# Row gathers that drop padding places by a bounds check, in a two-layer graph network on one core

## What is computed

```
h = relu(layernorm(x))                            # layer 0: attention, 2 heads of 64
feat = (h @ W).reshape(N, 2, 64)
e = leaky_relu(el[src] + er[dst]); alpha = softmax of e over the edges of one dst
x = x + layernorm(segment_sum(feat[src] * alpha, dst) + bias)
h = relu(layernorm(x))                            # layer 1: three hops
agg = h
for _ in range(3):
    att = sum((agg[head] @ q_w) * tanh(rel * agg[tail] @ k_w))     # head = src, tail = dst
    agg = normalized segment_sum(softmax(att) * rel * agg[tail], head)
    out = out + agg + h
x = x + out
```

## Time and profile before

| | |
|---|---|
| median of 3 runs | 9552.52 us (9550.24 to 9559.58) |
| the profiled execution: its own time, its span | 9554.53 us, 9552.7 us |
| busy share of the span, PE / DVE / ACT / POOL | 84% / 81% / 78% / 71% |
| row gathers on POOL | 6832 indirect DMAs |
| DMA engines, mean busy share in the hops | 0.54 |

### The profile page before, as it was taken

How to read it: one execution, slowest core, us unless ns; L and a number is a source line. 1 busy time by engine, 2 the same in 40 slices (tenths; PEclk the granted TensorE clock), 3 DMA queues, 4 the chain that set the end, 5 groups by cost and what they waited for, 6 DMA issues and landing times.

```text
span 9552.7 us, 271679 instructions
## 1 busy us (share of the span) xinstructions
PE 7999.1 (84%) x62097; PEld 6935.3 (73%) x62097; DVE 7758.0 (81%) x33664; ACT 7498.1 (78%) x24462; POOL 6812.7 (71%) x7069
## 2 busy tenths in 40 slices
PE   8977777777776888888887888888887888888887
PEld 7866666666665777777776777777776777777776
DVE  8989999999997777777777777777777777777776
ACT  6739999999986777777777777777777777777776
POOL 2347777777775777777776777777776777777776
PEclk9989999999998999999998999999998999999999
DMA  2014444444444555555555555555555555555555
GB/s 55 5 35 108 108 108 110 108 108 108 108 113 132 157 161 156 159 157 158 161 155 167 157 158 159 157 161 156 159 159 163 161 156 159 158 158 161 156 160 147
DMA packets 1127114, 1309.11 MB, mean 137 GB/s; under 512 B 446660, under 2 KB 840730, under 8 KB 1126716
## 3 DMA queue, kind: packets, MB, share of 16 engines
q1 hardware_dynamic: 896038, 843.26, 28.7%
q0 software_dynamic: 229264, 460.98, 19.0%
q10 hardware_dynamic: 1670, 3.16, 0.1%
HBM read 1041.61 MB, written 261.38 MB: 136 GB/s over the span
## 4 chain that ended last, share of the span: by engine, by line
PE 35%; DMA 21%; issue 15%; DVE 12%; POOL 10%; ACT 4%; SPq 1%; DVEq 1%; POOLq 0%; ACTq 0%
PE bank L782 27%; DMA agg<-agg_d,arena 18%; POOL agg L744 10%; PE bank L959 3%; PE bank L944 3%; PE bank L912 2%; DVE agg L1689 2%; DVE agg L1679 2%; DVE arena L1788 2%; ACT arena L1100 2%; DMA agg<-feat_d,arena 1%; ACT arena L1180 1%; DVE arena L1765 1%; DVE arena L1669 1%; DVE arena L1647 1%
## 5 line engine op out<-in xcount | busy, mean ns | idle before, releaser
L744 POOL DMA_INDIRECT agg<-agg_d,arena x5124 | 4871.6, 951 | 1687.1 <-issue 1380.6
L1788 DVE TENSOR_TENSOR arena<-agg,bank 128x256 f32<-128x256 f32 x2562 | 1079.8, 421 | 1404.7 <-DMA agg<-agg_d,arena 1184.5
L782 PE MATMUL bank<-arena 128*128 128x129 f32 x10248 | 1763.1, 295 | 305.1 <-ACT arena L1180 297.8
L744 POOL DMA_INDIRECT agg<-feat_d,arena x1708 | 1619.5, 948 | 532.1 <-issue 418.5
L782 PEld LDWEIGHTS bank<-arena 128*128 128x128 f32 x10248 | 1378.9, 195 | 434.5 <-issue 409.4
L1176 ACT ACTIVATE arena<-arena 128x1 f32<-128x1 f32 x2562 | 755.4, 295 | 1158.1 <-DVE arena L1653 1121.8
L782 PE MATMUL bank<-tmp,wide 128*128 128x256 f32 x5124 | 1577.9, 391 | 6.4 <-DMA wide<-left_d 6.4
L782 PE MATMUL bank<-tmp,kw_s 128*128 128x256 f32 x5124 | 1567.3, 388 | 0.1
L959 PE MATMUL bank<-ident,arena 128*128 128x128 f32 x5124 | 1027.3, 283 | 509.6 <-DVE arena L1788 506.6
L959 PEld LDWEIGHTS bank<-ident,arena 128*128 128x128 f32 x5124 | 695.4, 144 | 932.4 <-DVE arena L1788 709.3
L1171 ACT ACTIVATE arena<-agg,arena 128x256 f32<-128x256 f32 x2562 | 1342.4, 524 | 17.6 <-DVE arena L1781 12.1
(11 more groups left out here) (251 smaller groups left out, 16728.2 us busy)
## 6 DMA issues: line engine op xcount, KB each, us to landing
state_d<-arena SPq DMA_DIRECT2D x488, 455.0 KB
arena<-key_d SPq DMA_DIRECT2D x489, 448.0 KB
arena<-type_d SPq DMA_DIRECT2D x367, 448.0 KB
wide<-left_d SPq DMA_DIRECT2D x2562, 64.0 KB
agg<-agg_d,arena POOLq DMA_INDIRECT x5124
agg<-feat_d,arena POOLq DMA_INDIRECT x1708
arena<-er_d SPq DMA_DIRECT2D x854, 1.0 KB
arena<-peers SPq DMA_DIRECT2D x489, 7.0 KB
```

The lines of the kernel that those rows point to most:

```text
L744: nc.gpsimd.indirect_dma_start(out=rows_r[:, k % R, c, 0:width], out_offset=None, in_=table, in_offset=bass.IndirectOffsetOnAxis(ap=peer_r ...
L782: return nc.tensor.matmul(out, lhsT, rhs, start=start, stop=stop)
L1788: V.tensor_tensor(val_r[:, j % R, :, 0:F], rows_r[:, j % R, :, 0:F], bank[0][:, 0:G].rearrange("p (c f) -> p c f", c=2), ALU.mult).then_in ...
```

## The change

Padding places that are put behind the edges keep a real peer in one place of eight (KEPT = 8). In the other seven the peer field is filled with ones, which gives peer 8191, beyond the last node 6249. The row gathers get a bounds check at N - 1 that drops such rows instead of reporting an error. `decode` no longer clamps the peer number to 6249. The 86 padding places of layer 0 hold peer 7168 and are dropped too. A dropped row leaves in `rows_r` what stood there; a memset of the whole ring, once, makes that finite.

```
+KEPT = 8
+        filler_made = sem("filler_made")
+        filler_spread = sem("filler_spread")
...
-            sp.wait_ge(rowid_made, 1)
+            sp.wait_ge(filler_spread, 2)
             sp.dma_start(sorted_edges[0][WINDOWS * G:].rearrange("(l w) o -> l (w o)", l=1), sentinel[:, 0:G]).then_inc(prefilled, 16)
             sp.dma_start(sorted_edges[1][NB * REGION:NB * REGION + G].rearrange("(l w) o -> l (w o)", l=1), filler[0:1, :]).then_inc(prefilled, 16)
...
+            sp.wait_ge(rowid_made, 1)
             for at in range(0, U * SW, NG):
...
                         nc.gpsimd.indirect_dma_start(
                             out=rows_r[:, k % R, c, 0:width], out_offset=None, in_=table,
                             in_offset=bass.IndirectOffsetOnAxis(ap=peer_r[:, k, c:c + 1], axis=0),
+                            bounds_check=N - 1, oob_is_err=False,
                         ).then_inc(q["gathered"][k % R], 16)
...
             V.tensor_copy(iota16[:], colid[:, 0:CAP])
+            dve.wait_ge(filler_made, 2)
+            for i in range(1, KEPT):
+                last = V.tensor_scalar(filler[:, i:G:KEPT], filler[:, i:G:KEPT], MASK, None, ALU.bitwise_or)
+            last.then_inc(filler_spread, 1)
+            for i in range(1, KEPT):
+                last = V.tensor_scalar(sentinel[:, i:G:KEPT], sentinel[:, i:G:KEPT], MASK, None, ALU.bitwise_or)
+            last.then_inc(filler_spread, 1)
...
-                    do(V.tensor_scalar(s_peer, s_field, float(N - 1), None, ALU.min))
+                    do(V.tensor_copy(s_peer, s_field))
...
-                    do(V.tensor_scalar(s_peer, s_other, float(N - 1), None, ALU.min))
+                    do(V.tensor_copy(s_peer, s_other))
...
                 if s == 0:
+                    do(V.memset(rows_r, 0.0))
                     do(V.memset(acc_r[:, U - 1:U, :], 0.0))
```

More of the change, by code:

```diff
@@ L589, in _ @@
             nc.gpsimd.iota(giota[:], [[1, NG]], base=0, channel_multiplier=0, allow_small_or_imprecise_dtypes=True)
-            nc.gpsimd.iota(filler[:], [[1, G]], base=0, channel_multiplier=STRIDE)
-            nc.gpsimd.iota(sentinel, [[1, G]], base=PADKEY << SHIFT, channel_multiplier=0)
+            nc.gpsimd.iota(filler[:], [[1, G]], base=0, channel_multiplier=STRIDE).then_inc(filler_made, 1)
+            nc.gpsimd.iota(sentinel, [[1, G]], base=PADKEY << SHIFT, channel_multiplier=0).then_inc(filler_made, 1)
             nc.gpsimd.iota(biota[:], [[1, 64]], base=0, channel_multiplier=0, allow_small_or_imprecise_dtypes=True)
```

## The result

The change makes the kernel slower. Its median is 9953.61 us (9950.37 to 9954.97, 4 runs) against 9551.38 us for the kernel before (4 runs). The ratio is 1.0421, with an interval of 1.0409 to 1.0434: 402 us, 4.2%. The forecast was 9554 us within 9500 to 9800, so that the time lies above the range. The profiled execution has a span of 9948.5 us, 395.8 us more than before.

A forecast was written before the change was run, and what follows sets the result against it. The prediction took POOL's 6832 row gathers, one every 1.256 us, to bound the kernel. Check, dropped rows and register move counted 0 and the memset 1.7 us: 9554.5 + 1.7 = 9556.2 us profiled, 9554 us in the median, range 9500 to 9800.

The forecast's parts named there:

- What sets the pace: POOL's row gathers in layer 0 and the hops: one every 1.256 us, 6832 in all; each nanosecond is 6.8 us.
- The bounds check: On POOL's row gathers: taken to cost 0, with bounds of 0 and 727 ns a gather (4967 us).
- the test costs POOL time: Rival: testing 128 indices a gather lengthens POOL's work by 16 to 32 ns, 9664 to 9773 us or more; chance 0.30.
- 0.5 us to spare: The rest of a step takes 2.0 us against POOL's 2.5 us, so DVE can catch up late landings.
- does not enter: Row width (528 or 512 B) was said not to affect gather time: medians 944 and 945 ns, shortest 940 in both.
- Rows dropped: Dropping 10827 padding rows a hop: taken to gain 0 on POOL, upper bound 240 us.
- a dropped row saves POOL its share: Rival: fewer rows shorten POOL's gathers; 9494 us for a quarter, 9314 us for all; chance 0.24, including a DMA engines' gain.
- estimate of 28 us: Within the dropped-row rival: 13.7 ns per extra row on each of 16 engines, giving 28 us gain, 9526 us.
- The DMA engines gain: Within the dropped-row rival's 0.24: DMA engines set more of the pace, so 5% less traffic gains at most 59 us.
- L1788's wait falls: Sign that only the DMA engines gain: DVE's 1184.5 us wait for landed rows falls while the stretches do not.
- The register move: 6832 moves on POOL's sequencer, hidden behind the previous gather: cost 0; 198 us uncovered, a rival with chance 0.06.
- Start, decode, memset: Start instructions cost 0 (2.7 us at most), decode's copy for a clamp 0, the ring's memset 1.7 us.

The follow-up runs named there:

- e7: The kernel before, without a check, with 60 bodies in the hops in place of 61, so 84 fewer gathers; 9444.11 us, ratio 0.989.
- e1: The kernel before with the bounds check at 6249 on the row gathers alone, padding keeping real peers, no row dropped; 9952.45 us, ratio 1.0422.
- e6: The changed kernel with DVE's masks of layer 0 moved from ahead of the minimum to the head of the step; 9930.03 us, ratio 1.0403.
- e2: The changed kernel with the bound at 3124 in place of 6249, dropping about half of all rows; 9965.19 us, ratio 1.0435.
- e4: The kernel before plus 60 single gathers at its end: 16, 64 or 128 rows in four check forms; one execution, 9751.34 us including them.
- e8: The kernel before with a satisfied wait and a semaphore increment on POOL's sequencer ahead of each step's second gather; 9549.28 us, ratio 1.0.

## Why the prediction was wrong

**What sets the pace: right for a gather that gets longer.** Row gathers set the time, and each ns more on them counts 6.8 us. The 53 ns by which the mean hop gather grew are 90.5 us a stretch, and the hops lost 89.7 to 90.8. e7 shows the same from the other side: 84 gathers fewer are 106.1 us.

**The bounds check: the step that failed.** "I take 0: the instruction is the same one with the same operands but for the bound, and so nearest to itself." It costs 52 ns a gather on POOL, 355 us for 6832, and 402.6 us with what it set off (e1: 9952.45 - 9549.83). The argument took the likeness of two instructions for a likeness of their work. The rival "the test costs POOL time" had the mechanism, the place (nothing beside POOL hides it) and the sign (a median above 945), and had a chance of 0.30. Its price was mis-sized too: 16 to 32 ns, from one register instruction, where it was 52. Work that POOL does for a gather of 128 rows is not bounded by one register instruction of 32 ns. With 52 ns that sum gives 9554 + 355 = 9909 us; the other 44 are layer 0's 39 and the one ns by which the hops' mean rose more than their median.

**The range.** Its lower end rested on rivals that give nothing, its upper on the 32 ns. The sum had bounds of 0 and 727 ns, and the text put 0.07 above 9800. With POOL without slack and no row for the check, more of the chance belonged above.

**Layer 0's extra: not foreseen.** The prediction priced a gather and multiplied. 39 us of the loss are gathers that meet DVE's instructions at another place than before (e6). The 0.5 us to spare that it read for a step hold in the hops alone: in layer 0 DVE is busy 2082.59 of 2146.50 us, 2.44 us of each step of 2.51. The prediction's phrase that the row's width "does not enter" holds still: the shortest and the median are the same with both tables.

**Rows dropped: 0, right.** e1 (none dropped), the changed kernel (5%) and e2 (half) have the same 992/997 ns. The rival that a dropped row saves POOL its share (9494 or 9314 us) falls, and so does its estimate of 28 us from the spread of rows over the engines: between e1 and the changed kernel there are 1.2 us, the wrong way. On POOL a row is worth 0.75 ns (e4), where the bound was 7.4, and even that is not saved for a dropped one. That many descriptors can be made before the added cost shows, as the Trainium skill has it in "DMA: Bandwidth & Descriptors", section on the anatomy of one DMA, agrees with 84 ns for 112 more rows on 872. The count of 10827 rows a hop was near: the 16.51 MB less, at 4 B for a dropped row, are 10806 rows a hop and layer 0's 86. The filler's row b starts at 124 b, and not at 126 b as the description of the padding has it; nothing here hangs on that.

**The DMA engines gain: no.** "L1788's wait falls" was the sign of it. It rose to 1468.5 us, and with half of the bytes gone it was 1420.1, against 1444.6 with none gone (e1). Rows that land sooner did not shorten the stretches: POOL asked for the next ones at its own pace of 1.30 us.

**The register move: 0, right.** The gap stayed 0.30 us with 6832 moves of 29 ns; e8 adds that more sequencer work hides as well. The cover is larger than the one gather that the prediction named: the sequencer is 12.2 us ahead in the median.

**Start, decode, memset: small, as forecast.** The memset took 1.60 us for the 1.67 that was worked out, but the first gather came 0.8 us earlier, not 1.7 later, since DVE had reached the memset 2.5 us sooner. In e1, which has no memset, the first gather starts at 700.5 us, so such differences at the start are not the memset's; nothing measurable either way.

## What to carry to other kernels

Where one engine's instruction sets the pace with no slack, an option on that instruction has a price of its own until a row or a run shows otherwise; measure that option alone first, since one such number (here 52 ns) is multiplied by thousands. Padding in this loop costs by the instruction, not by the row: 28 gathers less per hop gave 106 us, some 10800 rows less per hop gave nothing. And when a pacing instruction changes its length, look at the mean beside the median: here the difference showed how often it now meets another engine's instructions.

## What the runs showed of the hardware

- The dropping bounds check costs POOL 52 ns of 944 in the loop, 26, 21 and 41 ns alone with 16, 64 and 128 rows; the form that reports an error costs 50, 46 and 74 ns alone.
- A dropped row takes no packet out of the queue's count (229264 with none, 5% and half dropped) and leaves 4 B of its 512 in its packet (460.98, 444.47 and 228.70 MB). It saves POOL nothing. With half of 128 rows dropped, a DMA's rows land 0.6 us sooner.
- Of a gather of 128 rows, 84 of 956 ns come with the last 112 rows; with 16 rows it takes 872 ns already. In the loop 0.30 us between two gathers come on top.
- POOL's sequencer runs ahead of POOL: a register move starts 12.2 us (median) ahead of the gather that it belongs to.
- In layer 0 of the changed kernel each of the 223 gathers that start 0.10 to 0.30 us behind the running minimum (two operands in SBUF) took 0.05 to 0.26 us longer than the median. None of the 88 less than 0.05 us behind it did, and none of the 620 behind an instruction with an operand in PSUM was 0.05 us longer. In the kernel before, 464 gathers start 0.05 to 0.10 us behind the minimum; there the minimum takes 0.53 us for 0.48, and the gather is not longer.
- DVE's masks, which read one tile in SBUF and a number for each partition (L1651, in the hops L1650 too), also lengthen gathers that start within about 0.15 us behind them, by up to 0.10 us in layer 0 and 0.13 us in the hops. The 36 us by which the changed kernel's hop gathers exceed their median stand behind these two.
